# The softmax normalisation of a window attention stage, moved from GpSimd to VectorE

## The reference, cut to what is computed

```
pos = depthwise_conv3x3(x, pos_w)              # x = x + pos + pos_b
win = affine1(x) cut into windows of 8 x 8     # N = 64 positions a window, 16 channels
q, k, v = win @ qkv_w.T + qkv_b                # 2 heads of 8 channels, q scaled by 8 ** -0.5
attn = softmax(q @ k.T, axis=-1)               # 64 x 64 for each window and head
out = (attn @ v) @ proj_w.T + proj_b
x = x + out
x = x + gelu(affine2(x) @ fc1_w.T + fc1_b) @ fc2_w.T + fc2_b
```

## Time and profile before

| what | value |
|---|---|
| median of the runs | 37019.83 us (3 runs, 37004.03 to 37028.43) |
| the profiled execution, its own time | 37018.4 us |
| its span in the profile | 37016.7 us |
| TensorE busy over the span | 34207.8 us (92%) |
| VectorE busy | 31945.6 us (86%) |
| ScalarE busy | 24888.2 us (67%) |
| GpSimd busy | 7323.3 us (20%) |
| instructions | 498647 |

### The profile page before, as it was taken

How to read it: one execution, slowest core, us unless ns; L and a number is a source line. 1 busy time by engine, 2 the same in 40 slices (tenths; PEclk the granted TensorE clock), 3 DMA queues, 4 the chain that set the end, 5 groups by cost and what they waited for, 6 DMA issues and landing times. The chain is left out here.

```text
span 37016.7 us, 498647 instructions
## 1 busy us (share of the span) xinstructions
PE 34207.8 (92%) x171926; PEld 25100.8 (68%) x171926; DVE 31945.6 (86%) x34733; ACT 24888.2 (67%) x28002; POOL 7323.3 (20%) x5452
## 2 busy tenths in 40 slices
PE   9999999999998998998999899899989989989999
PEld 6777777767777776777777777677777767773333
DVE  7777777779999999999999999999999999993202
ACT  6666666667777777777777777777777777771010
POOL 2222222222111221211122121112112111212000
PEclk9999999999999999999999999999999999999999
DMA  1111111114444445444444544544454454449857
GB/s 22 19 19 19 19 19 19 19 39 87 87 88 100 87 87 102 87 87 96 93 87 87 102 87 87 101 87 87 87 101 87 87 101 87 87 91 356 257 172 246
DMA packets 1703783, 3403.97 MB, mean 92 GB/s; under 512 B 539056, under 2 KB 671152, under 8 KB 1702576
## 3 DMA queue, kind: packets, MB, share of 16 engines
q0 software_dynamic: 615040, 2229.56, 31.4%
q1 hardware_dynamic: 934576, 903.08, 8.9%
q10 hardware_dynamic: 154112, 270.62, 2.0%
HBM read 744.84 MB, written 497.03 MB: 34 GB/s over the span
## 5 line engine op out<-in xcount | busy, mean ns | idle before, releaser
L896 PE MATMUL surf_ps<-surf_parts,surf_matr 128*128 128x512 f32 x92480 | 22655.2, 407 | 2527.0 <-ACT surf_Bc L957 2331.1
L896 PEld LDWEIGHTS surf_ps<-surf_parts,surf_matr 128*128 128x128 f32 x92480 | 17959.7, 195 | 7222.8 <-issue 2633.8
L930 ACT ACTIVATE surf_rK<-surf_g 128x1024 f32<-128x1024 f32 x1360 | 1444.3, 1062 | 5612.5 <-DVE surf_g L1041 5612.5
L1215 PE MATMUL conv_ps<-conv_rows,conv_w 128*96 128x512 f32 x8256 | 3557.0, 593 | 135.9 <-DVE conv_rows L1236 83.0
L992 POOL DMA_DIRECT2D surf_p<-surf_q x1360 | 2623.7, 1929 | 4577.1 <-DVE surf_q L1057 4472.1
L442 POOL TENSOR_TENSOR att_pr<-att_pr,att_rs 128x1024 f32<-128x1024 f32 x1024 | 2142.8, 2093 | 5968.3 <-DVE att_rs L509 5968.3
L987 POOL DMA_DIRECT2D surf_nK<-surf_B x1360 | 1174.1, 863 | 9557.9 <-DVE surf_nK L1043 9370.1
L1215 PEld LDWEIGHTS conv_ps<-conv_rows,conv_w 128*96 128x96 f32 x8256 | 1345.5, 163 | 2347.0 <-issue 2337.7
L203 PEld LDWEIGHTS att_pv<-att_pt,att_vx 128*32 128x32 f32 x32768 | 1859.6, 110 | 795.5 <-ACT att_pt L334 684.0
L507 DVE TENSOR_REDUCE att_sm<-att_pr 128x16 f32<-128x1024 f32 x1024 | 1247.6, 1218 | 1331.4 <-ACT att_pr L341 1331.4
L998 POOL DMA_DIRECT2D surf_p<-surf_m x1360 | 1183.0, 870 | 6120.9 <-DMA surf_p<-surf_q 5796.6
(11 more groups left out here) (95 smaller groups left out, 53107.9 us busy)
## 6 DMA issues: line engine op xcount, KB each, us to landing
surf_nK<-surf_B POOLq DMA_DIRECT2D x1360, 512.0 KB, 4.5
surf_p<-surf_q POOLq DMA_DIRECT2D x1360, 512.0 KB, 5.6
surf_p<-surf_m POOLq DMA_DIRECT2D x1360, 512.0 KB, 4.5
conv_rows<-hidden SPq DMA_DIRECT2D x688, 256.0 KB, 4.0
hidden<-conv_outs ACTq DMA_DIRECT2D x688, 192.0 KB, 4.7
conv_us<-flowed SPq DMA_DIRECT2D x344, 256.0 KB, 8.3
conv_xs<-attended SPq DMA_DIRECT2D x344, 256.0 KB, 9.6
mixed<-conv_rows POOLq DMA_DIRECT2D x344, 256.0 KB, 6.8
```

Source lines behind the costliest of these rows:

```text
L896: mm = pe.matmul(ps[:, t, :], matr[:, mat, :], parts[:, par, part, t, off + 2:off + 2 + W], start=(i == 0), stop=(i == count - 1))
L1215: mm = pe.matmul(ps[b % 2][:, bb, :], w_sb[:, dx, :], rows[:, b, bb, dx:dx + W], start=(dx == 0), stop=(dx == 2))
```

## The change

In `attention_stage` the block of GpSimd is removed, and GpSimd does nothing in this stage. The same multiplication, with the same operands and the same semaphores, becomes a function of VectorE's block. VectorE's slot calls it directly behind each `total`. TensorE's and ScalarE's lists stay as they are, and so does everything outside this stage.

```diff
-        @block.gpsimd
-        def _(pool):
-            def norm(i, rg):
-                if not there(i):
-                    return
-                pool.wait_ge(rec_done, i * 4 + (rg + 1))
-                pool.tensor_tensor(pr[:, rg], pr[:, rg], rs[:, rg, :].unsqueeze(2).to_broadcast([P, WC * HEADS, N]),
-                                   ALU.mult).then_inc(norm_done, 1)
-
-            def slot(i, par):
-                norm(i, 1)
-                norm(i, 2)
-                norm(i, 3)
-                norm(i + 1, 0)
-
-            every_slot(pool, slot)
...
+            def norm(i, rg):
+                if not there(i):
+                    return
+                dve.wait_ge(rec_done, i * 4 + (rg + 1))
+                dve.tensor_tensor(pr[:, rg], pr[:, rg], rs[:, rg, :].unsqueeze(2).to_broadcast([P, WC * HEADS, N]),
+                                  ALU.mult).then_inc(norm_done, 1)
+
...
                 residual(i - 1, o)
                 total(i, 1)
+                norm(i, 1)
                 conv(i + 1, o, range(9, 10))
                 top(i, 2)
 
                 conv(i + 2, par, range(0, 1))
                 total(i, 2)
+                norm(i, 2)
                 top(i, 3)
                 conv(i + 2, par, range(1, 3))
 
                 total(i, 3)
+                norm(i, 3)
                 conv(i + 2, par, range(3, 5))
                 top(i + 1, 0)
                 conv(i + 2, par, range(5, 6))
 
                 conv(i + 2, par, range(6, 7))
                 total(i + 1, 0)
+                norm(i + 1, 0)
                 top(i + 1, 1)
```

## The result

The changed kernel takes 37212.39 us (median of 5 runs, 37203.37 to 37236.43), the kernel before 37015.1 us in the same session (5 runs, 37004.03 to 37028.43). The ratio is 1.0054, with a 95% interval from 1.004 to 1.0069: **slower by 197 us**, where + 136 us was forecast, at a time of 37155 in a range from 37060 to 37250.

What follows compares the result with a forecast made beforehand. TensorE, busy 988.6 of 1000 us in the attention stage, was taken as the bound. A delay of 0.53 us over 256 chunks gave + 136 us, so 37155 us, with 8 in 10 between 37060 and 37250.

Steps and rivals of the forecast that it cites:

- The wait for GpSimd goes: TensorE's 0.37 us wait per slot, before the first transpose of group 1, disappears; over 256 chunks that would be 95 us.
- The multiplication takes 1.22 us: Each multiplication moved to VectorE was put at 1.22 us, from a TENSOR_TENSOR of the same size; GpSimd's median is 1.90.
- D: How late VectorE's instructions behind the group 1 multiplication become: 1.25 to 1.32 us, taken as 1.27.
- The queue behind it: VectorE's subtraction of group 2, behind the group 1 multiplication, delays ScalarE's exponential by 1.27 us, then its copies and TensorE.
- The stretch of + 0.53 us a slot: TensorE's product with the values of group 1 starts 0.53 us later; the period goes from 31.5 to 32.0 us.
- The slack of 0.74 us: Part of D the queue can swallow: 0.64 us before ScalarE's second copy plus 0.10 before TensorE's product with the values.
- The other three at nothing: The multiplications of the groups other than group 1 were costed at nothing, covered by VectorE's idle time.
- the cover: VectorE's idle time before its sums, 5.2 us a chunk, plus 1.6 given back by collisions, against 5.1 us of multiplications.
- Rival A: The slack is there and only the wait for GpSimd goes: faster, 36924 us; chance 0.12.
- The sum: Attention stage's total cost over all chunks: + 0.53 x 256 = + 136 us.
- TensorE waits some 0.9 us a chunk: New waits for ScalarE's copies, before the second transpose and the values product of group 1: 0.37 + 0.53 us.
- Outside the stage nothing moves: Everything outside the attention stage was taken to keep its time, so no term was added for it.

Runs made afterwards that it cites:

- second run: The kernel before, multiplications still on GpSimd, with the addition that writes xs moved ahead of the sum of group 1: 36924.2 us (0.9974).
- seventh run: The changed kernel with group 1 kept on GpSimd, only groups 2, 3 and 0 multiplied on VectorE: 36953.69 us (0.9982 against the kernel before).
- fifth run: The kernel before with 40 memsets of one column added on VectorE in the set-up of attention: 36958.23 us (0.9983).
- third run: The changed kernel with the query product computed twice in each slot: 37076.49 us (1.0015 against the kernel before).
- first run: The changed kernel with the addition that writes xs moved ahead of the sum of group 1: 36916.81 us (0.9974 against the kernel before).

## Why the prediction was right, and what it missed

- *The wait for GpSimd goes.* Right. Its reason, the collision with the addition that writes xs, was shown by the second run.
- *The multiplication takes 1.22 us, D is 1.27.* Measured 1.225 and 1.26.
- *The queue behind it makes the exponential of group 2 late, and that passes through ScalarE to TensorE.* Right, and shown from three sides: one call moved takes the loss away, group 1 alone makes all of it, the other three make none. The stretch of + 0.53 us a slot was measured as + 0.50, in the slots without a drop. The slack of 0.74 us was read in a slot with the 0.37 us wait in it, but both readings give the same period: 1.27 - 0.37 = 0.90 us on top of the 31.13 of a slot without waits is 32.03.
- *The other three at nothing.* Right (the seventh run). VectorE's idle time before its sums, which was the cover, shrank from 5.2 us a slot to 3.3 (606.1 us in 184.5 slots); before the sum of group 1 it shrank from 2.51 to 1.70. Rival A took the rows to agree with a factor of about two between the engines; 1.90 against 1.225 us is a factor of 1.55.
- *What was mis-sized: the price of idle time.* The sum took a wait of TensorE at its length. "TensorE waits some 0.9 us a chunk" came true in the slot without a drop, with 0.94 (0.74 on average, because where TensorE is slow the second wait is gone), but I left out what TensorE's clock does behind it: the sum had no term for it, and gave no reason. The drops cost another 0.50 us a slot, 127 us in all. In no row of the steady slots of before was there a drop, with an idle time of 0.37 us; so nothing in them gave the price, but a kernel that lives at a granted clock of 1.00 has it to lose, and the range should have held that as a bound. The Trainium skill (TensorE: Matmul & The Clock Gate, section A second HAM failure mode: psum-queue depth-cycling) tells of a kernel in which short and frequent idle times between groups of matmuls let the clock swing between its two levels. The runs here agree: granted clock 0.66 over the 5 us behind a wait of 0.64 us, and no drop once the third run filled it.
- *"Outside the stage nothing moves."* Wrong, by - 61 us. The change adds instructions to VectorE's program ahead of the surface stage's loop, and the pause at the turn of that loop is shorter by 0.109 us; the fifth run gets a like gain from added instructions alone. By what mechanism they set the pause stays open.

In sum the runs give 128 (0.50 x 256) + 127 - 61 = 194 us, as by the spans; the medians give 197. The forecast had 136 for the first term and nothing for the other two. It was nearer than its parts: two errors of opposite sign, one twice the other. Without the second the time would have been near 37270 us, outside the range. The mechanism in the attention stage was right; that the time fell into the range is in part luck.

## What to carry to other kernels

An operation moved to an engine with spare time is to be priced by what is queued directly behind it, and by how many steps of other engines follow that without a pause; here one of four equal moves carried the whole loss, and putting one other instruction ahead of the wait took it back. Slack that is read in a slot with a wait in it shrinks by that wait when the wait goes. When a kernel is timed to a few tenths of a per cent, compare the stages whose code was not touched as well: a different number of instructions ahead of a loop was worth 62 us here, where the moved call of the second run was worth 91.

## What the runs showed of the hardware

- A wait of TensorE costs more than its length where the granted clock follows it down. After 0.63 and 0.64 us of idle time the clock held in one slot and fell in another; after 0.37 (before) and 0.29 us (first run) it did not fall in any steady slot. Filling the wait with a product that nobody needs saved 136 us (third run), although the added product itself makes TensorE's work longer. Why one slot drops and its neighbour not is open; it wasn't tried.
- VectorE's pause at the turn of the surface loop depends on the instructions that its program has ahead of it: 0.12 us with the changed kernel's, 0.14 with three groups' multiplications or with 40 memsets, 0.23 in the kernel before, 0.25 with 8 memsets, 0.35 with group 1's multiplications alone (medians over all turns). The memsets show that it is not the work that counts but the instructions ahead. Their number doesn't act in one direction: some ten more lengthen the pause, 30 to 40 more shorten it. By what mechanism is open.
- GpSimd's multiplication and a VectorE instruction with two inputs in SBUF hold each other up: 2.29 against 1.90 us for GpSimd's, 2.27 against 0.68 for VectorE's convolution step, and GpSimd's is back at 1.90 us once the addition on VectorE was moved away from it (second run).
